# Strassen query projections in a fused decoder: steps of the first and the last head group put in another order

## The reference, cut to what matters

```python
q = (hidden_states @ Wq.T).reshape(bsz, q_len, H, HD).transpose(0, 2, 1, 3)      # H = 32, HD = 128
k = (cross_attention_states @ Wk.T).reshape(bsz, kv_len, KVH, HD).transpose(0, 2, 1, 3)   # KVH = 8
v = (cross_attention_states @ Wv.T).reshape(bsz, kv_len, KVH, HD).transpose(0, 2, 1, 3)
q = _rmsnorm(q, q_norm_w)
k = _rmsnorm(jnp.repeat(k, GROUPS, axis=1), k_norm_w)                            # GROUPS = 4
scores = jnp.einsum('bhqd,bhkd->bhqk', q, k) * scale + mask
out = jnp.einsum('bhqk,bhkd->bhqd', softmax(scores), v) @ Wo.T
x = _layernorm(x + out)
```

## Time and profile before

| | us |
|---|---|
| median of 3 runs | 1008.18 |
| lowest and highest | 1007.4, 1011.13 |
| the profiled execution | 1011.42 |
| its span, first to last instruction | 1009.3 |
| PE busy | 955.8 |
| DVE, POOL, ACT busy | 639.5, 525.4, 487.4 |

### The profile page before, as it was taken

The page is one execution under the profiler, slowest core; times in us unless marked ns, Lnnn a source line. Parts: engine busy times, 40 slices in busy tenths (PEclk is TensorE's granted clock), DMA queues, the critical chain, the costliest instruction groups (busy, mean ns, idle before and its releaser), DMA issues.

```text
span 1009.3 us, 15661 instructions
## 1 busy us (share of the span) xinstructions
PE 955.8 (95%) x4926; PEld 788.5 (78%) x4926; DVE 639.5 (63%) x1421; ACT 487.4 (48%) x1358; POOL 525.4 (52%) x432
## 2 busy tenths in 40 slices
PE   4998999999999999878999999999999999999895
PEld 3766688788888887757888888888888888888682
DVE  4746553512221277567877878778778768678877
ACT  4656542412222347344555555654654645555454
POOL 4336533834352547465475575674663663855322
PEclk9999999999999999979999999999999999999997
DMA  6100122310111111010012020110110120110002
GB/s 217 65 20 2 41 86 84 105 63 11 52 62 62 63 42 35 22 43 22 1 43 63 17 62 26 42 49 14 42 52 10 42 62 0 42 52 12 0 2 83
DMA packets 18024, 45.69 MB, mean 45 GB/s; under 512 B 2176, under 2 KB 2816, under 8 KB 16704
## 3 DMA queue, kind: packets, MB, share of 16 engines
q1 hardware_dynamic: 17984, 45.20, 13.4%
HBM read 43.10 MB, written 2.10 MB: 45 GB/s over the span
## 4 chain that ended last, share of the span: by engine, by line
PE 74%; DVE 11%; POOL 5%; issue 5%; ACT 4%; DMA 1%; SPq 0%; POOLq 0%; DVEq 0%; ACTq 0%
PE bank L507 22%; PE bank L508 21%; PE bank L509 21%; PE bank L824 4%; PE bank L834 2%; DVE pb L2287 2%; ACT pb L1364 1%; POOL w_lo L1570 1%; POOL res L1688 1%; DVE q2t L2206 1%; PE bank L518 1%; DMA raw_a<-in_w_q 1%; PE bank L811 1%; DVE pt_lo L1930 1%; DVE bst L2117 1%
## 5 line engine op out<-in xcount | busy, mean ns | idle before, releaser
L507 PE MATMUL bank<-act_hi,w_hi 128*128 128x512 f32 x448 | 183.8, 410 | 4.3 <-issue 2.7
L509 PE MATMUL bank<-act_hi,w_lo 128*128 128x512 f32 x448 | 176.2, 393 | 0.0
L508 PE MATMUL bank<-act_lo,w_hi 128*128 128x512 f32 x448 | 176.2, 393 | 0.0
L1827 POOL TENSOR_TENSOR pb<-pb,prec 128x512 f32<-128x512 f32 x64 | 67.1, 1048 | 174.5 <-DVE prec L2296 174.5
L1570 POOL TENSOR_TENSOR w_lo<-raw_a,w_hi 128x512 fp32r<-128x512 f32 x101 | 130.4, 1303 | 48.7 <-ACT w_hi L1295 33.2
L1364 ACT ACTIVATE pb<-pb,nmax 128x128 f32<-128x128 f32 x256 | 99.4, 391 | 46.3 <-DVE nmax L2291 46.3
L507 PE MATMUL bank<-w_hi,ot_hi 128*128 128x512 f32 x256 | 106.7, 417 | 0.8 <-DVE ot_lo L1930 0.8
L507 PEld LDWEIGHTS bank<-act_hi,w_hi 128*128 128x128 f32 x448 | 85.1, 190 | 23.1 <-issue 7.0
L509 PE MATMUL bank<-w_hi,ot_lo 128*128 128x512 f32 x256 | 101.2, 395 | 0.0
L508 PE MATMUL bank<-w_lo,ot_hi 128*128 128x512 f32 x256 | 100.9, 394 | 0.0
L1570 POOL TENSOR_TENSOR h_lo<-hb,h_hi 128x512 fp32r<-128x512 f32 x28 | 37.5, 1338 | 120.4 <-ACT h_hi L1236 120.4
(11 more groups left out here) (233 smaller groups left out, 2336.5 us busy)
## 6 DMA issues: line engine op xcount, KB each, us to landing
raw_a<-in_w_gu SPq DMA_DIRECT2D x7, 1024.0 KB, 5.2
raw_a<-in_w_q SPq DMA_DIRECT2D x28, 256.0 KB, 3.4
raw_b<-in_w_kv SPq DMA_DIRECT2D x8, 512.0 KB, 3.3
raw_b<-in_w_dn SPq DMA_DIRECT2D x7, 512.0 KB, 3.4
raw_b<-in_w_o SPq DMA_DIRECT2D x7, 512.0 KB, 4.9
raw_a<-in_w_o SPq DMA_DIRECT2D x14, 256.0 KB, 4.0
res<-in_x SPq DMA_DIRECT2D x8, 256.0 KB, 6.3
raw_b<-in_ctx_t SPq DMA_DIRECT2D x8, 256.0 KB, 3.2
```

The costliest lines, as they stand in the source:

```text
L507: mm(o, l_hi, r_hi, start=first, stop=False)
L508: mm(o, l_hi, r_lo, start=False, stop=False)
L509: return mm(o, l_lo, r_hi, start=False, stop=last)
L1827: TT(pb[:, jj % 2, :, :], pb[:, jj % 2, :, :], prec[:, jj % 2, :].unsqueeze(2).to_broadcast([P, GH, L]), ALU.mult).then_inc(p_norm, 1)
```

## The change

It moves steps; nothing is computed that was not before.

- Group 0, ACT: `wp_hi(1, 1)` is done at the end of slot 0, behind `ot_evac`, and not in slot 1 behind `q_copy`.
- Group 0, POOL: in slot 1 `combine_t2` runs ahead of `wp_rest(1, 1)`; in slot 3 `combine_t4` runs ahead of `p_scale`.
- Group 0, DVE: in slot 0 `combine_t1` comes behind `pt_rest`; `t_rest` of t2 comes in slot 1 and of t1 in slot 2, each one slot sooner.
- All groups, DVE: in slots 0 and 1 `pt_rest` comes ahead of `q_part`.
- Last group: the fourth head's `q_square` and `q_part` are at the end of slot 1, not in slot 2; in slot 2 PE does `qs_step` ahead of `d_step`, DVE does `q_var` ahead of `softmax_max`, and POOL `q_rsqrt` ahead of `p_scale`. The `ln_stats`, `rsqrt` and `ln2` of the first three blocks come a slot later each.

```diff
--- before.py
+++ after.py
@@ -303,11 +303,15 @@
 
         def part_early(g, jj):
 
+            if is_last(g) and jj == 2:
+                return None
             return PART_NEXT.get(jj) or (PART_FIRST if first_group(g) else PART_EARLY).get(jj)
 
         def part_late(g, jj):
 
-            return (0, 1, 2) if first_group(g) and jj == 1 else PART_LATE.get(jj)
+            if jj == 1:
+                return (0, 1, 2) if first_group(g) else (0, 1, 3) if is_last(g) else None
+            return PART_LATE.get(jj)
 
         def swapped(gn, i):
 
@@ -879,6 +883,8 @@
                 if j == 3:
                     s_step(*turn)
                 pt_step(g, jj)
+                if j == 2 and is_last(g):
+                    qs_step(pg, pn)
                 if not before:
                     q_step(1, 3)
                 if before:
@@ -886,7 +892,8 @@
                 if j == 2:
                     if is_last(g):
                         kt_step(pg, pn)
-                    qs_step(pg, pn)
+                    else:
+                        qs_step(pg, pn)
                 pv_step(g, jj)
 
 
@@ -1411,7 +1418,8 @@
                     softmax_exp(*turn)
                 if make and jj == 1:
                     q_copy(g + 1)
-                    wp_hi(g + 1, jj)
+                    if not start:
+                        wp_hi(g + 1, jj)
                 if jj == 0 and not start:
                     for h in range(3 if is_last(g) else GH):
                         wo_hi(g, h)
@@ -1423,6 +1431,8 @@
                 if j == 2 and is_last(g):
                     kt_evac(pg, pn)
                 ot_evac(g, jj)
+                if start and jj == 0:
+                    wp_hi(1, 1)
                 if start and jj == 1:
                     t_round(t2, t2_raw, t_step, 10)
                 if start and jj == 2:
@@ -1841,10 +1851,14 @@
                 if make and jj == 4:
                     combine_u4(g + 1)
                 if first_group(g) and jj == 1:
+                    combine_t2()
                     wp_rest(1, 1)
-                    combine_t2()
+                if first_group(g) and jj == 3:
+                    combine_t4()
+                if j == 2 and is_last(g):
+                    q_rsqrt(pg, pn)
                 p_scale(*((g, jj + 1) if j < 3 else (pg, 4 * pn)))
-                if j == 2:
+                if j == 2 and not is_last(g):
                     q_rsqrt(pg, pn)
                 if first_group(g) and jj == 0:
                     combine_s(1)
@@ -1854,8 +1868,6 @@
                     else:
                         wp_rest(g + 1, 1)
                     combine_s1(g + 1)
-                if first_group(g) and jj == 3:
-                    combine_t4()
                 if jj == 7 and isinstance(g, int) and g == GROUPS - 2:
                     wo_rest(GROUPS - 1, 3)
                 if jj == 0 and not first_group(g):
@@ -1892,12 +1904,12 @@
             last = GROUPS - 1
             for jj in range(1, 4):
                 slot(last, jj, make=False)
-                rsqrt(23 + jj)
+                if jj > 1:
+                    rsqrt(22 + jj)
             for jj in range(4, 8):
                 if jj < 7:
                     p_scale(last, jj + 1)
-                if jj > 4:
-                    rsqrt(22 + jj)
+                rsqrt(22 + jj)
 
             def dl_sum(k):
 
@@ -2321,21 +2333,27 @@
                     v_rest(pg, pn, j + 1)
                 if j == 2:
                     k_var(pg, pn)
+                if j == 2 and is_last(g):
+                    q_var(pg, pn)
                 if j < 3 or is_last(g):
                     softmax_max(*turn)
                 if not before:
                     combine_t1_dif()
                     softmax_rec(*turn)
-                    combine_t1()
                 if j == 0:
                     v_rest(pg, pn, 1)
                 part = part_early(g, jj)
+                if jj < 2:
+                    pt_rest(g, jj)
+                if not before:
+                    combine_t1()
                 if part and jj < 7 and (make or jj < 3):
                     d, qn, qh = part
                     q_part(g + d, qn, qh)
                 if j == 3 and make:
                     q_add(g + 1, jj - 1)
-                pt_rest(g, jj)
+                if jj >= 2:
+                    pt_rest(g, jj)
                 if j == 2:
                     k_norm(pg, pn)
                 if j < 3 and make and jj > 1:
@@ -2350,13 +2368,13 @@
                     q_part(g + 1, 1, 0)
                 if j == 3:
                     softmax_rec(*turn)
-                if j == 2:
+                if j == 2 and not is_last(g):
                     q_var(pg, pn)
                 if make or jj < 3:
                     ot_rest(g, jj)
+                if start and jj == 1:
+                    t_rest(t2, t2_raw, 2, t_step, 12)
                 if start and jj == 2:
-                    t_rest(t2, t2_raw, 2, t_step, 12)
-                if start and jj == 3:
                     t_rest(t1, t1_raw, 4, t_step, 8)
                 if start and jj == 4:
                     t_rest(t4, t4_raw, 6, t_step, 14)
@@ -2472,8 +2490,8 @@
             def last_slot(jj):
 
                 ot_rest(last, jj - 1)
-                if jj == 4:
-                    ln2(26)
+                if jj < 6:
+                    ln2(21 + jj)
                 if jj < 7:
                     softmax_max(last, jj + 1)
                 else:
@@ -2481,7 +2499,7 @@
                     ln_stats(29)
                     gates_rank(0)
                 pt_rest(last, jj)
-                if jj > 4 and jj < 7:
+                if jj < 7:
                     dve.wait_ge(d_add, 8 * last + jj - 1)
                     ln_stats(22 + jj)
                 if jj < 7:
@@ -2497,11 +2515,11 @@
 
             for jj in range(1, 4):
                 slot(last, jj, make=False)
-                b = jj - 1
-                dve.wait_ge(d_add, 8 * last + b + 1)
-                ln_stats(24 + b)
-                if b:
-                    ln2(23 + b)
+                if jj == 3:
+                    ln2(24)
+                if jj > 1:
+                    dve.wait_ge(d_add, 8 * last + jj - 1)
+                    ln_stats(22 + jj)
             for jj in range(4, 8):
                 last_slot(jj)
             dve.wait_ge(d_add, 8 * last + 7)
```

## The result

The changed kernel took 991.27 us (median of 4 executions, 990.58 to 992.38) against 1007.94 for the kernel before (median of 4, 1007.4 to 1011.13): ratio 0.9829, interval 0.9807 to 0.9852. Compared once more, on one chip with seven executions of before, it took 989.77 against 1009.86: 0.9800 (0.9784 to 0.9817). The gain is 17 to 20 us. The profiled execution took 990.58 us with a span of 988.4, where before's took 1011.42 and 1009.3: 20.8 us less.

What follows compares the result with a forecast made beforehand. PE, busy 95% of the span, bounds the kernel, so only its waits and half clock can yield. 19.3 + 1.5 + 1.5 = 22.3 us off the profiled 1011.42 gives 989.1, off the median 1008.18 gives 985.9; range 982 to 992.

Steps and rivals of the forecast that it cites:

- A: Rival: the 2 us wait staying in slot 2 drops PE's clock again, costing 1.7 us: 987.6 us; chance 0.27.
- Slot 0, DVE: Group 0: pt_lo ends near 408.6, before PE is ready at 409.3; pv's wait and the half clock behind it go.
- ACT and POOL, t2: Group 0, slots 0 and 1: combine_t2 ends at 417.1; PE's 2.5 us wait for pb goes, 5 us to spare.
- t_rest a slot ahead: Group 0, slots 1 to 4: both `issue` waits (5.9 us) go; DVE limits slot 2, where 2.1 us of wait stay.
- combine_t4 costs nothing: Group 0, slot 3: combine_t4 ahead of p_scale(0,4) falls in POOL's idle time and frees slot 4; uncovered, 2.5 us once.
- First group: Group 0 loses 22.1 us; less 2.1 of wait in slot 2 and 0.7 of small waits, 19.3 us are gained.
- Loop groups: Slot 0 of six groups: pv's 0.17 us wait for pt_lo and a slower matmul go; 1.5 us gained (1.0 to 2.0).
- Last group: Earlier pt_rest, q_part moved to slot 1 and qr ready sooner gain 1.5 us, bounds -0.7 and 3.
- B: Rival: DVE and POOL hinder each other more, subtractions +1.0 and k_var +1.1: 988.0 us, or 989.7 with A; chance 0.12.
- C: Rival: both `issue` waits (5.9 us) stay, with half of the slow clock (4.5): 996.3 us; chance 0.08.
- D: Rival, slower: waits of about 2 us recur and the clock stays at half; 60 us of it gives 1016; chance 0.02.
- E: Rival: no wait stays in slots 2 to 4 of group 0: 983.1 us or a little less; chance 0.04.

Runs made afterwards that it cites:

- e5: Kernel before with one edit of group 0: pt_rest ahead of combine_t1 and q_part in slots 0 and 1; 1004.96 us, ratio 0.9952.
- e4: Changed kernel with, in slot 1 of group 0, the third head's token sum (q_square, q_part) ahead of t2's rounding and rest; 988.06 us, ratio 0.9794.
- e2: Kernel before with the edits of group 0 alone; 991.55 us, ratio 0.9834.
- e7: e4 with t_rest(t2) behind k_norm of slot 2 and, in slot 5 of group 0, pt_rest ahead of q_part; 987.19 us, ratio 0.9779.
- e11: Changed kernel with combine_t4 behind p_scale(0,4) again, as in the kernel before; 990.41 us, one execution.
- e9: e7 with POOL's rest of the weight block (w_lo) ahead of p_scale in slot 1 of groups 1 to 6; 986.60 us, ratio 0.9770.
- e12: Changed kernel with the last group's norm pieces (ln_stats, ln2, rsqrt of its first three blocks) back in their old slots; 992.73 us, one execution.

## Why the prediction came out as it did, point by point

The direction and the size hold: 985.9 us forecast, 991.27 measured. It lies inside the range, but only 0.7 us from its upper end, and above every price that I gave to a rival that came true (A, 987.6). The 5.4 us between forecast and result are 1.5 in the work forecast for the profiled execution (989.1 against 990.58) and 3.9 in the step from there to a median. The 1.5 flatter the working: 1.1 us of the profiled gain came ahead of the first moved step, by chance, so the work itself is about 2.5 short.

**Slot 0, DVE.** Right: pv(0,0) at 408.0 without a wait, and 4.5 us in slot 0 for 4.4 (e5), with 5.3 over the group.

**ACT and POOL, t2.** Right in time and order: combine_t2 from 410.93 to 415.96, w_lo until 417.23, p_scale(0,2) until 418.27, 4.5 us ahead of PE at 422.77.

**t_rest a slot ahead.** Right that both `issue` waits go, right that DVE becomes the limit of slot 2, and right in the size of the wait, 2.7 us against 2.1. But the way there was wrong in one term: I let the pair start behind ot_lo, at 420.5, and overlooked that it also waits for combine_t4_head: DVE stood 1.62 us in front of it, with the third and the fourth sum behind. That it came out near is luck in part, since the two subtractions were taken at 2.8 us and measured at 2.36. e4, which takes just that order away, got 1.9 us back in slot 2 against e2. By my working with the Trainium skill, "SBUF — State Buffer", section "Who interferes with whom", the pair would have taken 3.8 us. It began at 420.81 beside a POOL step that ran from 420.73 for 1.29 us, and took 1.08 us longer than the 1.28 it takes beside an idle POOL (e7): that is about what was left of the POOL step, and no other POOL step followed. The rule agrees with both rows; my working with it counted a second POOL step that wasn't there. One row of before doesn't fit it, the quick pair at 442.01: it took its 1.28 us beside a POOL step of a much smaller block:

```profile
441.45 2.90 POOL L1808 TENSOR_TENSOR qr<-qv,pow_m 128x16 f32<-128x16 f32 x1 [0.17 <-DVE qv L2263]
```

Not every POOL step holds DVE back, then; what sets this one apart was not tried.

**combine_t4 costs nothing.** Nothing in slot 3, right (10.35 us in after and in e11), but "frees slot 4" was left without a price: 0.9 us (e11, one execution).

**First group.** 19.3 us forecast, 17.6 measured between the two profiles. From pv(0,0) to slot 5's transposes after still takes 46.9 us (408.04 to 454.98), 4.5 more than the template's 42.4, where I had left 2.8: the wait in slot 2 is 0.6 longer, half clock adds 1.3 (rival A), and 0.5 of small losses stand for my 0.7. My 9.0 us for half clock in before was a remainder, what was lost less the waits. The pieces bear it out: 1.8 us in slot 0, 1.8 in slot 3, and in slot 2 19.00 less 5.2 of waits less the 8.8 that e2 takes there without wait or half clock, 4.9; 8.5 in all, and the rest is small losses that e2 has too. Two roundings were off by 0.1 and cancel: the loss is 22.0, not 22.1, and the wait by my own terms 2.0, not 2.1. One reading was wrong: the half clock of 440 to 449 doesn't follow the wait of 3.2 us. The granted clock is 0.58 in 439 to 440 already, and that wait began at 440.2; ahead of it stood the 1.8 and 0.2 us that rival A names.

**Loop groups.** 1.5 forecast, 0.7 between the profiles, and 0.8 between the means of the six profiles without the new order (424.8) and the seven with it (424.1, e9 left aside). The step that failed is that I priced slot 0 alone, and there too low (2.75 us, not 1.5), and took it for granted that PE could keep the time. 2.0 us of it went again in slots 1, where waits for the weight chain show for 1.2; that the chain is the cause of all of it is not shown.

**Last group.** 1.5 forecast, 1.46 measured, the same in every profile to 0.03. The waits are those announced: the fold for kraw 0.5 (0.7 forecast), the key transposes 1.1 (1.3), pt_lo 0.35 of 1.1 left. qr is ready at 924.5 in after, and softmax_max(7,4) asks for it at 928.3. e12 shows that the norm pieces carry it, by way of kraw.

**From the profiled execution to the median.** This is the step that failed most. I took the 3.2 us by which the profiled execution of before stood over its median off the forecast too. 1.4 of them were chance of another kind: the three executions of before on record had a median of 1008.18, all 31 one of 1009.6. The rest would not carry over if it belongs to the half clock of group 0, nearly all of which the change removes. The granted clocks of before fit that, but it is not shown, since the clock also has stretches at 0.50 elsewhere. After's profiled execution was not over its median but 0.7 us under it. Set against the median of all 31 executions of before, 1009.6, and of all eight of after, 990.7, the change brought 18.9 us.

**Rivals.** A, that the wait in slot 2 brings half clock, happened in three of five profiles, for 1.3 us in slot 2, not 1.7, and for 0.4 over group 0. B did not: k_var took 0.16 us, and the pair less than I had counted. C did not: both `issue` waits are gone. D did not: neither profile of the changed kernel has a stretch at 0.50 between slot 3 of group 0 and the end of the attention groups. My sign of being wrong, more than one stretch at 0.50 before 460, should have said where: after's profile has two, at 84 to 88 and at 429 to 433, and only the second lies in the changed part. E did not, though e7 comes near it.

A kernel that beats both is e9: 986.60 us, ratio 0.9770 (0.9754 to 0.9786) to before, with e7, which can't be told from it, at 987.19; e7 was measured beside after's 989.77.

## What to carry to other kernels

When a step is moved ahead, list all that it waits for, buffers that it overwrites among them, and all that is queued behind it: here the costly thing was not the moved step but the token sum, two short operations, that had to wait behind it. A gain at one place of a loop counts only as far as the next chain that doesn't follow the bound engine (here a load of weights) lets it: measure each slot by a landmark that every kernel has, not by the sum of waits. And before a forecast made on one profiled execution is carried over to a median, ask whether what makes that execution differ is in the part that the change removes.

## What was not expected of the hardware

The same wait of 2.5 us in front of the same instruction was followed by half clock in three of five profiles, and two profiles of one kernel had their stretches at 0.50 in other places with the same sum, 20.4 us. A stretch at 0.50 also came in six of the fourteen profiles near 84 to 89 us, far ahead of anything edited; here in after's, where before's shows 1.00 for the same window:

```profile
84.00:88.00 4.00, 4.00 (x10) 2.28 (x9) 2.82 (x4) 3.95 (x8) 3.43 (x3) 0.57 0.00 0
```

And 3.4 us at half clock cost PE 1.3 us in slot 2 of after, less than the half that I had reckoned with, but 1.8 in slots 0 and 3 of before. What makes the difference was not tried.
